# Layer-0 row maxima as rows: a transpose and four-row products in place of full-width products

## What is computed

```python
def _L0_xattn_ref(q, k, v, Wq, bq, Wk, bk, Wv, bv, Wo, bo):
    qh = (q @ Wq.T + bq).reshape(B, S, H, Hd).transpose(0, 2, 1, 3)
    kh = (k @ Wk.T + bk).reshape(B, S, H, Hd).transpose(0, 2, 1, 3)
    vh = (v @ Wv.T + bv).reshape(B, S, H, Hd).transpose(0, 2, 1, 3)
    scores = jnp.einsum('bhqd,bhkd->bhqk', qh, kh) / jnp.sqrt(jnp.float32(Hd))
    attn = jax.nn.softmax(scores, axis=-1)
    out = jnp.einsum('bhqk,bhkd->bhqd', attn, vh)
    return out.transpose(0, 2, 1, 3).reshape(B, S, D) @ Wo.T + bo
...
x = x + _L0_xattn_ref(_layernorm(x, axis=-1), ctx_1024, ctx_1024, ...)
x = x + _L0_ffn_ref(_layernorm(x, axis=-1), ...)     # router: norms, affinities, argmax, ranks
```

## Time and profile before

| | us |
|---|---|
| median of 3 runs | 951.37 |
| lowest and highest run | 950.8, 953.16 |
| profiled execution | 950.98 |
| its span, first to last instruction | 949.3 |
| of it before the first `scores` (layer 0's start) | 22.6 |
| of it the 32 iterations, up to the start of the last `scores` | 22.6 to 238.4 |
| of it the rest of routing, to the first expert products | to 262 |
| of it experts | to about 395 |
| of it layer 1 | to 949.3 |

### The profile page before, as it was taken

How to read it: one execution, slowest core, us unless ns; L and a number is a source line. 1 busy time by engine, 2 the same in 40 slices (tenths; PEclk the granted TensorE clock), 3 DMA queues, 4 the chain that set the end, 5 groups by cost and what they waited for, 6 DMA issues and landing times.

```text
span 949.3 us, 28567 instructions
## 1 busy us (share of the span) xinstructions
PE 858.2 (90%) x10216; PEld 683.9 (72%) x10246; DVE 692.0 (73%) x1957; ACT 431.5 (45%) x1010; POOL 484.3 (51%) x992
## 2 busy tenths in 40 slices
PE   2998899998679997799999999999999999999973
PEld 1666566666469886587878878787888878888752
DVE  2777787888533555468888888888878888887865
ACT  1555555555225654234454544445444454544432
POOL 5454577878532223334555546455454655645241
PEclk9999999999679999899999999999999999999995
DMA  7664400000456653021121212112121211212120
GB/s 211 223 239 185 185 13 19 13 11 15 132 165 161 164 156 95 15 55 33 35 58 33 61 36 59 37 34 62 33 60 36 55 41 34 63 33 56 27 54 10
DMA packets 57982, 71.37 MB, mean 75 GB/s; under 512 B 8050, under 2 KB 34546, under 8 KB 57842
## 3 DMA queue, kind: packets, MB, share of 16 engines
q1 hardware_dynamic: 43842, 45.48, 18.7%
q10 hardware_dynamic: 11952, 19.86, 5.6%
q0 software_dynamic: 2048, 4.20, 1.5%
HBM read 45.13 MB, written 24.38 MB: 73 GB/s over the span
## 4 chain that ended last, share of the span: by engine, by line
PE 80%; DVE 10%; issue 3%; DMA 2%; ACT 2%; POOL 1%; SPq 0%; ACTq 0%; POOLq 0%; DVEq 0%
PE psum L1569 8%; PE psum L1499 7%; PE psum L1586 7%; PE psum L1548 7%; PE psum L1490 6%; PE psum L1528 6%; PE psum L853 4%; PE psum L1574 4%; PE psum L843 3%; PE psum L1597 3%; PE psum L354 3%; PE psum L359 3%; PE psum L371 2%; PE psum L1559 2%; PE psum L378 1%
## 5 line engine op out<-in xcount | busy, mean ns | idle before, releaser
L1744 ACT ACTIVATE a_pT<-psum 128x512 f32<-128x512 f32 x128 | 69.5, 594 | 54.8 <-PE psum L1574 54.8
L459 ACT ACTIVATE l_pT<-psum 128x512 f32<-128x512 f32 x128 | 72.9, 598 | 40.4 <-PE psum L359 35.4
L1499 PEld LDWEIGHTS psum<-a_cTm,a_Wk 128*128 128x128 f32 x512 | 63.5, 196 | 30.0 <-issue 27.2
L1341 POOL TENSOR_TENSOR f_hd<-f_hmc,f_wmean 128x1 f32<-128x1 f32 x32 | 6.7, 211 | 151.6 <-DVE f_hr L2002 151.6
L573 DVE TENSOR_REDUCE l_mx<-psum 128x4 bf16<-128x512 f32 x128 | 81.9, 681 | 1.2 <-PE psum L345 1.0
L1889 DVE TENSOR_REDUCE a_mxf<-psum 128x4 f32<-128x512 f32 x128 | 81.1, 674 | 1.4 <-PE psum L1559 1.4
L1569 PE MATMUL psum<-a_qT,a_kT 64*128 64x128 f32 x1024 | 75.3, 287 | 5.1 <-ACT a_v L1766 1.1
L1499 PE MATMUL psum<-a_cTm,a_Wk 128*128 128x128 f32 x512 | 74.7, 291 | 3.4 <-POOL a_cTm L1298 2.7
L1490 PEld LDWEIGHTS psum<-a_xT,a_Wq 128*128 128x128 f32 x512 | 64.5, 192 | 15.2 <-issue 14.3
L1569 PEld LDWEIGHTS psum<-a_qT,a_kT 64*128 64x128 f32 x1024 | 63.0, 190 | 14.6 <-issue 14.2
L1877 DVE TENSOR_TENSOR a_kT<-psum,a_nkm 128x512 f32<-128x512 f32 x64 | 42.5, 664 | 40.7 <-PE psum L1499 40.7
(11 more groups left out here) (298 smaller groups left out, 2211.3 us busy)
## 6 DMA issues: line engine op xcount, KB each, us to landing
sorted_x<-r_zeros ACTq DMA_DIRECT2D x12, 1408.0 KB, 5.9
a_r_all<-a_r_rows SPq DMA_DIRECT2D x64, 256.0 KB, 4.1
e_w<-in_E_W1b SPq DMA_DIRECT2D x39, 258.0 KB, 2.8
e_xt<-sorted_x SPq DMA_DIRECT2D x39, 64.0 KB, 2.4
sorted_y<-e_yt ACTq DMA_DIRECT2D x39, 64.0 KB, 2.6
a_cin<-in_ctx SPq DMA_DIRECT2D x32, 64.0 KB, 3.8
out<-f_x SPq DMA_DIRECT2D x32, 64.0 KB, 3.3
x_res<-in_x SPq DMA_DIRECT2D x1, 512.0 KB, 5.6
```

Source lines behind the costliest of these rows:

```text
L459: nc.scalar.activation(pT[:, k, :], tp[k], ACT.Exp, scale=SCALE).then_inc(exp_ready, 1)
L1499: last = nc.tensor.matmul(bank[:, i * S:(i + 1) * S], Wk[:, 4 * half + i, :], cTm[:, b % 2, :], start=True, stop=True)
L1744: nc.scalar.activation(pT[:, 2 * half + e, :], tp[e], ACT.Exp, scale=SCALE).then_inc(exp_ready, 1)
```

## The change

The diff, cut to the parts that do something in the loop:

```diff
@@ tensor_part @@
-            for k in range(Q4):
-                pe.wait_ge(mx_ready, 4 * b + k + 1)
-                for j in range(Q4):
-                    h = Q4 * k + j
-                    last = nc.tensor.matmul(tp[k][:, j * S:(j + 1) * S], mx[:, b % 2, h:h + 1].to_broadcast([P, P]),
-                                            negI[:], start=False, stop=(j == Q4 - 1))
-                last.then_inc(t_done, 1)
+        def max_rows(b):
+            pe.wait_ge(mx_ready, 4 * b + 4)
+            for k in range(Q4):
+                last = nc.tensor.matmul(maxp[1][R * k:R * k + Q4, 0:S], mx[:, b % 2, Q4 * k:Q4 * k + Q4], identb[:],
+                                        start=True, stop=True, skip_group_check=True)
+            last.then_inc(mt_done, 1)
+
+        def minus_max(b):
+            pe.wait_ge(mxT_ready, b + 1)
+            if b == 0:
+                pe.wait_ge(cst, consts["rows_ready"])
+            for j in range(Q4):
+                for k in range(Q4):
+                    mm = nc.tensor.matmul(tp[k][:, j * S:(j + 1) * S], row_sel[R * k:R * k + Q4, j, :], mxT[R * k:R * k + Q4, :],
+                                          start=False, stop=(j == Q4 - 1))
+                    if j == Q4 - 1:
+                        mm.then_inc(t_done, 1)
...
@@ places @@
-            if q < B // G - 1:
+            if q < B // G - 2:
+                pe.wait_ge(rsem["num"], G * q + 5)
+            elif q == B // G - 2:
                 pe.wait_ge(rsem["xnT"], G * q + 5)
...
@@ PE's loop @@
             scores(b)
-            if b >= 8 and b % G == 0:
-                places((b - 8) // G)
+            max_rows(b)
             if b >= 4:
                 affinity(b - 4)
             if b == 0:
                 expert_sums()
             else:
                 back_transposes(b - 1, 1 - s)
+            minus_max(b)
+            if b >= 8 and b % G == 0:
+                places((b - 8) // G)
             if more:
                 x_transpose(b + 2, s)
...
@@ scalar_part @@
+        def max_copy(b):
+            act.wait_ge(mt_done, b + 1)
+            wait(act, t_done, 4 * b)
+            nc.scalar.copy(mxT[:], maxp[1][0:R * (Q4 - 1) + Q4, 0:S]).then_inc(mxT_ready, 1)
...
             s, first, more = b % 2, b == 0, b + 2 < B
+            max_copy(b)
             exps(b, s, 0)
@@ make_consts @@
+    def rows_part(g):
+        ident, row4 = c["ident"], c["row4"]
+        nc.gpsimd.tensor_tensor(row4[:], ident[:, 0:4], ident[:, 32:36], ALU.add).then_inc(ready, 1)
+        for i in (2, 3):
+            g.wait_ge(ready, 9 + i)
+            nc.gpsimd.tensor_tensor(row4[:], row4[:], ident[:, 32 * i:32 * i + 4], ALU.add).then_inc(ready, 1)
+        g.wait_ge(ready, 13)
+        nc.gpsimd.tensor_scalar(c["row_sel"][:], row4[:].unsqueeze(2).broadcast_to([P, 4, P]), -1.0, None, ALU.mult).then_inc(ready, 1)
```

More of the change, by code:

```diff
@@ L66, in routing_state @@
         zeros=sb("zeros", [P, 704]))
-    s = {n: sem(n) for n in ("w_in", "set", "wsq", "wsum_done", "wsum", "wn", "rs2", "den", "xn2", "xnt", "xnT",
+    s = {n: sem(n) for n in ("w_in", "set", "wsq", "wsum_done", "wsum", "rs2", "den", "xn2", "xnt", "xnT",
                              "num_done", "num", "choice", "place_done", "place", "z_out", "scat")}
@@ L108, in attention_routing_block @@
     mx = sb("l0_mx", [P, 2, H], BF16)
+    mxT = sb("l0_mxT", [R * (Q4 - 1) + Q4, S], BF16)
     pT = sb("l0_pT", [P, 4, Q4 * S])
@@ L174, in pool_part @@
     def pool_part(g, after_setup, before_last):
-        nc.gpsimd.memset(v[:, :, :, HD:], 1.0).then_inc(ones_set, 1)
+        nc.gpsimd.memset(v[:, :, :, HD:], 1.0).then_inc(cst, 1)
         g.wait_ge(w_in, N_W)
@@ L252, in pool_part @@
         x_norm(1, 1)
+        consts["rows_part"](g)
         setup_rest()
@@ L341, in max_scores @@
             wait(pe, mx_ready, 4 * b + 2 * u)
+            if u == 0:
+                wait(pe, mxT_ready, b)
             for j in range(Q4):
@@ L502, in vector_part @@
         dve.wait_ge(w_in, N_W)
-        dve.wait_ge(ones_set, 1)
+        dve.wait_ge(cst, consts["v_ones"])
         def x_stats(b, s):
@@ L677, in pool_part @@
             nc.gpsimd.tensor_tensor(c["mask4"][:], c["mask4"][:], c["mask"][:, 4 * i:4 * i + 4], ALU.add).then_inc(ready, 1)
+    def rows_part(g):
[6 more added lines that the diff above has]
+        nc.gpsimd.tensor_scalar(c["row_sel"][:], row4[:].unsqueeze(2).broadcast_to([P, 4, P]), -1.0, None, ALU.mult).then_inc(ready, 1)
     c["n_ready"] = 9
+    c["v_ones"] = 10
+    c["rows_ready"] = 14
     c["pool_part"] = pool_part
+    c["rows_part"] = rows_part
     return c
@@ L1131, in attention_ffn_block @@
     x4 = fb("x4", [P, 2, D])
-    w_in, p_set, nv_set, setup_done = sem("w_in"), sem("p_set"), sem("nv_set"), sem("setup_done")
-    sa_done, sa_read = sem("sa_done"), sem("sa_read")
+    w_in, p_set, setup_done = sem("w_in"), sem("p_set"), sem("setup_done")
+    NV_SET, SA_READ, MASKS = 4, 5, 6
+    sa_done = sem("sa_done")
     cin_ld = [sem(f"cin_ld{s}") for s in range(2)]
@@ L1346, in null_weights @@
             nc.gpsimd.tensor_tensor(wT[:, b % 2, :], nullT[:], rT[:], ALU.mult).then_inc(wT_ready, 1)
-        g.wait_ge(setup_done, 1)
+        g.wait_ge(setup_done, MASKS)
         null_keys(0)
@@ L1415, in prepare @@
                     nc.vector.tensor_copy(nv_blocks[rows, first:first + 3 * (P + G) + 1:P + G],
-                                          nv_col[rows, :].broadcast_to([HD, Q4])).then_inc(nv_set, 1)
+                                          nv_col[rows, :].broadcast_to([HD, Q4])).then_inc(setup_done, 1)
         def tensor(self, pe, bank_free):
@@ L1423, in tensor @@
                 nc.tensor.matmul(psum[:, 7, h_:h_ + 5:4], WqT[:, p, :], nk[:], start=True, stop=True)
-            pe.wait_ge(nv_set, 4)
+            pe.wait_ge(setup_done, NV_SET)
             for p in range(NP):
@@ L1437, in wait_free @@
         def wait_free(self, pe):
-            pe.wait_ge(sa_read, 1)
+            pe.wait_ge(setup_done, SA_READ)
         def masks(self, dve, part):
@@ L1447, in tensor_part @@
         pe.wait_ge(*before[0])
-        pe.wait_ge(setup_done, 1)
+        pe.wait_ge(setup_done, MASKS)
         def first_transpose():
@@ L1715, in scalar_part @@
         act.wait_ge(w_in, N_W)
-        act.wait_ge(setup_done, 1)
+        act.wait_ge(setup_done, MASKS)
         def first_context():
```

11 lines of the change are left out of this document (6 added, 5 removed).

## The result

The changed kernel takes 965.77 us (median of 4 runs, 964.16 to 973.8) against 952.26 us for the kernel before (median of 4, 950.8 to 953.92): a ratio of 1.0163, 95% interval 1.0137 to 1.0189. It is slower: by 13.5 us between the medians, by some 15 us by the ratio. The profiled execution took 966.27 us, span 964.3 us, against 950.98 and 949.3. The time lies outside the stated range of 948 to 964.

A forecast was written before the change was run, and what follows sets the result against it. Layer 0 was taken as bound by PE in plain iterations, ACT with the DMA, DVE with `places`. Terms +1.9, -1.7, +2.1 and +2.0 gave +4.3 us: 955.3 on the profiled execution, 955.7 as median; range 948 to 964.

The forecast's parts named there:

- The sign: Whole kernel: slower, 955.7 us forecast; chance of slower 0.58, same 0.27, faster 0.15.
- the path of a plain iteration: Plain iterations of layer 0: late exponentials, then ACT without a gap to `o_copy`, then the output product at 4.43 us.
- PE's products: PE, each iteration: `max_rows` 0.20 and `minus_max` 0.40 us replace L359's 0.91, giving PE 0.31 us.
- The third rival: PE: products don't overlap or mode changes drain the array; exponentials 0.25 to 0.5 us later still, 963 to 970; chance 0.10.
- Plain iterations: Layer 0 loop without DMA or `places`: 6.52 us instead of 6.42, because ACT's exponentials start later.
- the sum: Whole kernel: the terms for iterations, the wait of `places` and the clock together, +4.3 us.
- Iterations with the DMA: Layer 0 iterations where ACT issues a clearing DMA: issue hidden behind the third exponential, 6.53 us against 6.77.
- The fourth rival: Iterations with the clearing DMA: its issue isn't hidden, 8 x 0.5 = +4.0 us, 959.7; chance 0.16.
- The wait of `places`: Six iterations with `places`: it now waits for `num_copy`, so DVE's `locate` starts 0.35 us later, +2.1 us.
- The clock: Iterations with `places`: longer PE gaps bring one or two further clock falls, 1.5 x 1.34 = +2.0 us.
- Start-up: Start of the kernel: POOL's four small operations and b = 0's exchange of roles cost nothing.

The follow-up runs named there:

- e5: The changed kernel with the row products (`minus_max`) ahead of the back-transposes instead of behind them: 968.38 us, ratio 1.0173.
- e1: The changed kernel with the affinity behind `places` again in the six iterations, `places` not waiting for `num_copy`: 968.94 us, ratio 1.015.
- e2: The changed kernel with two unused 128 x 512 products on PE ahead of `places` in the six iterations: these take 8.8 to 9.2 us each.
- e4: The kernel before with one unused 128 x 512 product on PE ahead of `places` in the six iterations: 949.94 us, ratio 0.9985.
- e12: e10 with 4, 6 and 12 unused 128 x 128 products in PE's three waits behind the loop: 946.68 us, ratio 0.9924.
- e3: The changed kernel's order with the old 16 full-width products, without `max_rows`, `max_copy` and the row products: 959.09 us, ratio 1.0102.
- e9: The changed kernel with the two loops of the row products exchanged, so one bank's four stand together: 975.14 us, ratio 1.0193.
- e10: e4 with the clearing DMA's issue moved on ACT from ahead of the fourth exponential to behind `k_copy`: 948.09 us, ratio 0.9926.
- e8: e7 with, outside iterations with `places`, `x_transpose` ahead of the row products and `x_copy` ahead of the exponentials: 961.79 us, ratio 1.0100.
- e7: e6 with the row products also ahead of the back-transposes, as in e5: 953.06 us, ratio 1.0019.
- e6: e1 with one unused 128 x 512 product on PE ahead of `places` in the six iterations: 959.08 us, ratio 1.0079.

## Why the prediction was wrong

The sign was right, and so were the mechanisms and their places, but for the path of a plain iteration; the size was not, and the median lies 2 us outside the range.

- **PE's products.** Forecast 0.20 and 0.40 us, measured 0.15 and 0.33. The third rival didn't come: `max_rows`, with a change of tiling mode on both sides, takes 0.15 us, and what the rival charged, 0.25 to 0.5 us an iteration, is not there. The changes are not free either: the affinity and the back-transposes, which now stand between them, take 0.25 and 0.57 us between starts, where it was 0.19 and 0.50. From `scores` to `x_transpose` PE takes 2.37 us instead of 2.67, so it gets 0.30 us, where 0.31 was forecast: too much was allowed for the products, and nothing for the changes. The Trainium skill, TensorEngine Tiling (Array Packing), section Key Properties, says that changing the tiling mode drains TensorE; the trace shows some 0.06 us at each of these two, and no wait as long as a product.
- **Plain iterations.** Forecast 6.52, measured 6.62. The path that I had wrong is the last piece: I let it run through `o_copy`, which came at 4.07 us, before the forecast 4.11. It runs through `x_copy` and the projections, which start 3.76 us behind `scores` and take 0.77 us to the output product, where I had given them 0.68; so the output product starts at 4.53, not 4.43. 14 iterations: +2.8 us, where 1.5 was in the sum for 15. That the late exponentials set the length is shown by e5, which starts the exponentials 0.4 us earlier and takes 6.27.
- **Iterations with the DMA.** Forecast 6.53 with the issue hidden, measured 6.62 and hidden: -1.5 us against -2.0. The fourth rival didn't come. In the changed kernel they are no longer than the plain ones: the sequencer issued the DMA at 67.30, ahead of `x_copy`, the third exponential and `o_copy`, which stand before it in the program. The Trainium skill, TensorE: Matmul & The Clock Gate, section Architectural detail: the array is 16× 32×32, not 1× 128×128, gives ScalarE a queue of 8 instructions in strict order. The trace agrees as far as three waiting instructions go; no run here tests the eight.
- **The wait of `places`.** Forecast 0.35 us in each, measured 0.59 of DVE's idle time in five and 0.46 in b = 8: I had put `num_copy`'s release of PE at 0.05 us, and PE's first product starts 0.26 us behind its end (172.42 to 172.68), in b = 8 0.15. e1 took the wait away and brought two such iterations to 8.56 and 8.36.
- **The clock, the step that failed.** In the sum it stood as 1.5 further falls at 1.34 us. It fell in all six, four more than before, and in five of them for 6.8 us instead of 3.4. The six iterations cost 12.1 us more; taking off the wait (6 x 0.6) and what plain ones lost too (6 x 0.2) leaves about 7, where 2.0 was in the sum. I took the price from b = 16 of the kernel before, though I had worked out that PE's gaps would be longer, and then counted the falls low. The loop of the kernel before has no fall of 6.8 us that could have given the price. e2 shows the cause: the same waits with PE kept busy, no fall, 1.0 to 2.0 us less for each.
- **Start-up.** b = 0 to 2 took 2.1 us more, where I had put almost nothing. The 1.2 us of b = 0 need not be the change's: in e4, whose loop up to b = 7 is the kernel before's, b = 0 took 9.31 us against 7.77, and 8.97 in the changed kernel. The products run at the lower level there at first: the 16 of L359 take 1.89 us in b = 0 of both, 1.07 later. (The clock column of the tables reads 1.00 there all the same, so in b = 0 it can't be relied on.) The projections' pairs take 0.39 us from 28.04 in the kernel before, and still 0.64 at 28.56 in e4: when the clock rises differs between executions.

What stays open: but for e12's fills, the program behind the loop is the same in all kernels, and from the last `scores` on it took 712 us in the profiled executions of both kernels, but 710 (e3) to 721 (e9) in the experiments. In e2 the clock over the first 25 us of layer 1 was 0.54, in the changed kernel 0.85. So part of the differences in total between the experiments comes from behind the loop. It doesn't look like chance alone: without the row products that part took 709 to 713 us in five traces (the kernel before, e3, e4, e10, e12), with them 715 to 721 in eight of nine, the changed kernel's own being the ninth. Whether the row products lengthen it, and how, is not shown. I rely on the lengths of the iterations for the causes, from one trace of each kernel, and they account for the loop alone.

## What to carry over

A faster form of an operation pays only if its result isn't released later: read at what time the next engine starts, not how long the own engine works. A faster product ahead of a wait also lengthens the wait, as e3 against the changed kernel shows. When a change lengthens an idle stretch of PE, price the fall of the clock behind it in every such stretch, and give the price a range: the 1.34 us taken here lie in the lower part of the 1.0 to 2.0 us that came. And look at each moved instruction's whole list of waits: both the wait for `num_copy` here and the one of e8 were harmless in their old place.

## What the runs showed of the hardware

- Sixteen products with four contraction rows each, on four row groups, take 0.33 us between starts, and nearly the same (0.37) when the four of a group stand in a row; 16 full-width products of the same 128 columns take 0.91. So the products overlap in either order.
- Full-width products beside a change of tiling mode take some 0.06 us longer between starts: the affinity 0.25 instead of 0.19, the back-transposes 0.57 instead of 0.50.
- A wait of PE of 1.0 to 1.2 us was followed by a fall of the clock in some iterations and not in others of the same kernel (two of six before, four of six in e1); with 1.25 to 1.47 us it fell in five of six (e3), with 1.57 to 1.96 in all six. It stayed at 1.2 GHz for 3.4 or 6.8 us, and the wait's length alone doesn't tell which: 6.8 behind 1.57 us (b = 12), 3.4 behind 1.72 (b = 8).
- Useless products in such a wait cost little and can keep the clock: with two of 128 x 512 in e2 none of six falls was left, with one in e4 neither of two, with one in e7 none; with one in e6 three of six remained, one of them with no wait left ahead of `places`.
- ACT's sequencer issues a DMA while an earlier exponential still runs, if that comes ahead of it in order: 0.54 us of issue cost nothing in the changed kernel (67.30) and 0.35 us per iteration in the one before (6.77 against 6.42 in e10).
